# Third layer of a four-layer pair network: powers of the unscaled matrix, later lay-out copies, and a convolution border applied on VectorE

## What is computed

```
# layer 1 (the convolution and the output map; all of it linear after the windows are chosen)
g = conv3x3_same_depthwise(v, dw_w) + dw_b
out = einsum(attention_out + g, wo_w) + wo_b
# layer 2 for each image row: P = 128 positions, D = 64 channels
corr = xhat @ xhat.T / (D - 1 + 1e-6)
A = corr * (mask of the 9 largest of each row)
A = 0.5 * (A + A.T) + eye
deg = clip(A.sum(-1), 1e-6); dinv = deg ** -0.5
A = dinv[:, None] * A * dinv[None, :]
f(y) = alpha * (I - A) @ y + (A @ y) @ theta.T
y = 8 steps of a fourth-order Runge-Kutta on f;  return relu(y)
```

## Time and profile before

| | us |
|---|---|
| median of 3 runs | 1153.05 |
| lowest and highest of them | 1147.65 and 1153.18 |
| the profiled execution | 1148.3 |
| its span, first to last instruction | 1146.5 |
| layer 1, from its first product to the end of its statistics | 380.0 to 474.7 |
| layer 2, from its first product to its last lay-out sum | 478.5 to 1088.0 |

### The profile page before, as it was taken

How to read it: one execution, slowest core, us unless ns; L and a number is a source line. 1 busy time by engine, 2 the same in 40 slices (tenths; PEclk the granted TensorE clock), 3 DMA queues, 4 the chain that set the end, 5 groups by cost and what they waited for, 6 DMA issues and landing times. The chain is left out here.

```text
span 1146.5 us, 25390 instructions
## 1 busy us (share of the span) xinstructions
PE 1064.3 (93%) x9446; PEld 761.2 (66%) x9446; DVE 756.4 (66%) x3598; ACT 525.2 (46%) x1115; POOL 348.0 (30%) x481
## 2 busy tenths in 40 slices
PE   5888999999997899769999999999999999999788
PEld 3436888888886344447677776777767677776576
DVE  3685888888886322356766767667676766766268
ACT  2485777777775100125344444444445444453200
POOL 0154666666664100001212212122221212212231
PEclk9998999999999799779999999999999999999879
DMA  8000000000000000000000000000000000000012
GB/s 170 1 0 2 3 3 2 3 3 3 3 3 2 1 1 1 10 1 1 1 2 1 1 1 2 1 1 2 1 1 1 2 2 1 2 1 1 0 41 110
DMA packets 10317, 11.04 MB, mean 10 GB/s; under 512 B 3668, under 2 KB 8020, under 8 KB 10196
## 3 DMA queue, kind: packets, MB, share of 16 engines
q1 hardware_dynamic: 8820, 8.84, 3.0%
q10 hardware_dynamic: 1376, 0.59, 0.3%
HBM read 5.14 MB, written 4.19 MB: 8 GB/s over the span
## 5 line engine op out<-in xcount | busy, mean ns | idle before, releaser
L1557 PE MATMUL quad<-theta,nat 128*128 128x512 f32 x512 | 240.7, 593 | 0.0
L1356 POOL TENSOR_TENSOR nat<-nat,const 128x512 f32<-128x512 f32 x32 | 40.7, 1271 | 437.8 <-DVE nat L1495 437.8
L737 POOL TENSOR_TENSOR nat<-nat,arena 128x512 f32<-128x512 f32 x128 | 131.5, 1049 | 40.9 <-DVE arena L795 37.1
L1565 PEld LDWEIGHTS quad<-flat 128*128 128x128 f32 x768 | 104.9, 191 | 46.4 <-ACT flat L1387 25.1
L1557 PEld LDWEIGHTS quad<-theta,nat 128*128 128x128 f32 x512 | 87.5, 191 | 61.7 <-issue 61.7
L1565 PE MATMUL quad<-flat 128*128 128x128 f32 x768 | 124.2, 284 | 2.8 <-ACT flat L1387 1.7
L795 DVE CUSTOM_DVE_ANT_0 nat<-quad,arena 128x128 f32<-128x128 f32 x512 | 111.3, 283 | 1.5 <-PE quad L881 1.4
L1387 ACT ACTIVATE flat<-quad 128x256 f32<-128x256 f32 x192 | 73.6, 384 | 70.2 <-PE quad L1565 56.6
L754 ACT ACTIVATE nat<-bank 128x512 f32<-128x512 f32 x128 | 73.2, 599 | 65.1 <-PE bank L889 65.1
L1464 DVE SCALAR_TENSOR_TENSOR flat<-nat,c,duo 128x128 f32<-128x128 f32 x64 | 22.1, 345 | 102.7 <-PE duo L1574 102.7
L889 PE MATMUL bank<-const,nat 128*128 128x128 f32 x512 | 73.3, 276 | 8.1 <-ACT nat L754 8.1
(11 more groups left out here) (393 smaller groups left out, 2279.6 us busy)
## 6 DMA issues: line engine op xcount, KB each, us to landing
out<-nat SPq DMA_DIRECT2D x16, 256.0 KB, 2.0
const<-in_constants ACTq DMA_DIRECT2D x1, 400.5 KB, 3.3
arena<-in_L_conv_Ws SPq DMA_DIRECT2D x1, 240.0 KB
flat<-arena SPq DMA_DIRECT2D x3, 32.0 KB, 4.1
nat<-in_x SPq DMA_DIRECT2D x4, 0.2 KB, 12.1
arena<-in_L_conv_Wq ACTq DMA_DIRECT2D x1, 32.0 KB, 6.4
arena<-in_L_conv_Wk ACTq DMA_DIRECT2D x1, 32.0 KB, 6.1
arena<-in_L_conv_Wv ACTq DMA_DIRECT2D x1, 32.0 KB, 5.8
```

Source lines behind the costliest of these rows:

```text
L737: pool.tensor_tensor(scored, scored, of_head(least[b], h).broadcast_to([128, ROWS, L]), ALU.subtract).then_inc(lowered, 1)
L1356: pool.tensor_tensor(quarters(rem), quarters(rem), ident.unsqueeze(1).broadcast_to([128, ROWS, 128]), ALU.add).then_inc(diag_added, 1)
L1557: return pe.matmul(m.quad[:, n, :], vT[:, col(n)], m.theta[:, part, :], start=(part == 0), stop=False, skip_group_check=True)
L1565: last = pe.matmul(m.quad[:, row, place * C:(place + 2) * C], a8[g % 2][:, col(row)], zs[half][k % 2][:, n, :], start=False, stop=(k == 2) ...
```

## The change

Layer 1: the small products leave `close`. Instead, TensorE turns the eight border vectors into columns of bank 6 once, together with the bias (eight products more, ahead of `sides(2)`), VectorE copies them out, and for every bank, ahead of its statistics, VectorE subtracts the side columns in SBUF (128 x 8 elements), with two operations more for the first and the last bank.

Layer 2: write M for the unscaled matrix and D for the degrees. The kernel works with M and D^-1 in place of D^-1/2 M D^-1/2. `a1` is M with each row divided by the degree, `h2` = M D^-1 M and `h4` are the plain powers that ScalarE copies, and `a2`, `a4`, `a8` are the same divided by the degree, made on VectorE (from `h2` in SBUF), GpSimd (from `h4` in SBUF) and VectorE (from PSUM, in ScalarE's place). The turn of the scaled matrix (L1687) and the second scaling (L1541) go. GpSimd multiplies y by D^1/2 ahead (a `yn` of 128x256), and `weigh` on VectorE multiplies the result by D^-1/2. `final` is replaced by `sum_up`, two products of 64 columns for each half that accumulate onto `m.quad`, and one pair of transposes for both halves late in the step; `finish` is then two operations of 128x256. On TensorE `cor` goes ahead of `v12`, and the last `theta` goes between the first two `horner` rounds. GpSimd's `lay` comes a step later, behind the ready `a2`.

```diff
+            step(dve.tensor_copy(border, B[6][:, NWIN:NWIN + 8]))
+            step(dve.tensor_reduce(border_row, border[:, 2:8].rearrange("p (t x) -> p t x", t=2), AX.X, ALU.add))
+            sides_out = border[:, 0:2].unsqueeze(1).broadcast_to([128, 4, 2])
...
+                of_columns = out_rows(g).rearrange("p (r c) -> p r c", c=L)
+                step(dve.tensor_tensor(of_columns[:, :, 0:L:L - 1], of_columns[:, :, 0:L:L - 1], sides_out, ALU.subtract))
+                if g in (0, BANKS - 1):
+                    e = g // (BANKS - 1)
+                    outermost = of_columns[:, 3 * e, :]
+                    step(dve.tensor_scalar(outermost, outermost, border_row[:, e:e + 1], None, ALU.subtract))
+                    corners = border[:, 2 + 3 * e:5 + 3 * e:2]
+                    step(dve.tensor_tensor(outermost[:, 0:L:L - 1], outermost[:, 0:L:L - 1], corners, ALU.add))
                 dve.bn_stats(m.stats[:, 6 * g:6 * g + 6], out_rows(g))
...
                     pe.matmul(bank_of(g)[:, :], middle[:, i, :, :], m.x1[:, 4 * g:4 * g + 4, 1:1 + L],
-                              start=False, stop=False, skip_group_check=True)
-                    for dx, column in ((0, 0), (2, L - 1)):
-                        last = pe.matmul(bank_of(g)[:, column:column + 3 * L + 1:L], col_rows[:, dx, :, :], minus[:, 1:5],
-                                         start=False, stop=True, skip_group_check=True)
-
-                    if g in (0, BANKS - 1):
-                        e = g // (BANKS - 1)
-                        for dx in range(3):
-                            last = pe.matmul(bank_of(g)[:, e * 3 * L:(e * 3 + 1) * L], edge_rows[:, e, dx, :, :],
-                                             minus[:, dx:dx + L], start=False, stop=True, skip_group_check=True)
-                    last.then_inc(S("conv_made"), 1)
+                              start=False, stop=True, skip_group_check=True).then_inc(S("conv_made"), 1)
 
...
+            pe.wait_ge(S("edges_ready"), 1)
+            for n, rows in enumerate([col_rows[:, dx, :, :] for dx in (0, 2)] + [edge_rows[:, e, dx, :, :] for e in range(2) for dx in range(3)]):
+                last = pe.matmul(B[6][:, NWIN + n:NWIN + n + 1], rows, ident[C:C + 1, C:C + 1], start=True, stop=True)
             last.then_inc(S("bias_turned"), 1)
             for dx in range(3):
                 sides(2, dx)
...
+            for s in range(-1, GROUPS + 3):
                 p, c, r, a = stage(s)
+                if 0 <= s - 3 < GROUPS:
+                    pool.wait_ge(yn_weighed, min(s, GROUPS))
+                    if c is not None:
+                        pool.wait_ge(a2_ready, c + 1)
+                    lay(s - 3)
+                    pool.wait_ge(laid, s - 2)
+                if c is not None:
...
+                    pool.tensor_tensor(quarters(a4[c % 2]), quarters(h4), square_inv.unsqueeze(2).broadcast_to([128, ROWS, L]),
+                                       ALU.mult).then_inc(a4_ready, 1)
...
                     pool.wait_ge(rem_ready, p + 1)
                     pool.tensor_tensor(quarters(rem), quarters(rem), ident.unsqueeze(1).broadcast_to([128, ROWS, 128]),
                                        ALU.add).then_inc(diag_added, 1)
-                if r is not None:
...
+                    pool.wait_ge(dsq_ready, p + 1)
+                    fresh = quarters(yn[p % 2])
+                    pool.tensor_tensor(fresh, fresh, dsq.unsqueeze(2).broadcast_to([128, ROWS, C]), ALU.mult).then_inc(yn_weighed, 1)
...
-                    act.activation(a2, B[0][:, :], ACT.Copy).then_inc(a2_ready, 1)
+                    if c > 0:
+                        act.wait_ge(a4_made, c)
+                    act.activation(h2, B[0][:, :], ACT.Copy, scale=0.5).then_inc(h2_ready, 1)
...
-                    if c >= 2:
-                        act.wait_ge(final_made[1], c - 1)
-                    act.activation(a4[c % 2], B[0][:, :], ACT.Copy).then_inc(a4_ready, 1)
+                    if c > 0:
+                        act.wait_ge(a8_made, c)
+                        act.wait_ge(a4_ready, c)
+                    act.activation(h4, B[0][:, :], ACT.Copy).then_inc(h4_ready, 1)
...
-                    act.wait_ge(a8_made, c + 1)
-                    act.activation(a8[c % 2], B[0][:, :], ACT.Copy).then_inc(a8_ready, 1)
...
-            def finish(g, half):
-
-                dve.wait_ge(final_made[half], g + 1)
-                dve.scalar_tensor_tensor(out=held[half], in0=yT[g % 4][:, col(half)], scalar=m.c0[:, :], in1=B[3][:, 0:L],
-                                         op0=ALU.mult, op1=ALU.add).then_inc(held_ready[half], 1)
-                dve.wait_ge(held_ready[half], 2 * g + 1)
-                dve.tensor_tensor(held[half], held[half], B[3][:, L:2 * L], ALU.add).then_inc(held_ready[half], 1)
-                dve.wait_ge(held_ready[half], 2 * g + 2)
-                dve.scalar_tensor_tensor(out=x_of(g, half), in0=held[half], scalar=0.0, in1=x_of(g, half),
-                                         op0=ALU.max, op1=ALU.add).then_inc(x3_ready[half], 1)
+            def weigh(g, half):
+
+                dve.wait_ge(summed, 2 * g + half + 1)
+                if g > 0:
+                    dve.wait_ge(final_made, g)
+                dve.tensor_tensor(weighed[half].rearrange("p (n x) -> p n x", n=HALF), m.quad[:, HALF * half:HALF * (half + 1), 0:C],
+                                  dinv[g % 4][:, HALF * half:HALF * (half + 1)].unsqueeze(2).broadcast_to([128, HALF, C]),
+                                  ALU.mult).then_inc(weighed_ready, 1)
+
+            def finish(g):
+
+                dve.wait_ge(final_made, g + 1)
+                dve.scalar_tensor_tensor(out=held, in0=yT[g % 4], scalar=m.c0[:, :], in1=B[3][:, 0:PAIR],
+                                         op0=ALU.mult, op1=ALU.add).then_inc(held_ready, 1)
+                dve.wait_ge(held_ready, g + 1)
+                dve.scalar_tensor_tensor(out=x_of(g), in0=held, scalar=0.0, in1=x_of(g),
+                                         op0=ALU.max, op1=ALU.add).then_inc(x3_ready, 1)
+
+            def by_degree(t):
+                return t.unsqueeze(2).broadcast_to([128, ROWS, L])
 
             for s in range(-1, GROUPS + 2):
                 p, c, r, a = stage(s)
+                if c is not None:
+                    dve.wait_ge(h2_ready, c + 1)
+                    if c > 0:
+                        dve.wait_ge(v34_made, c)
+                    dve.tensor_tensor(quarters(a2), quarters(h2), by_degree(square_inv), ALU.mult).then_inc(a2_ready, 1)
...
-                    finish(r, 0)
+                    weigh(r, 0)
...
-                    finish(r, 1)
+                    weigh(r, 1)
...
+                if c is not None:
+                    dve.wait_ge(a8_made, c + 1)
+                    if c >= 2:
+                        dve.wait_ge(horner_made[1], 3 * (c - 1))
+                    dve.tensor_tensor(quarters(a8[c % 2]), quarters(B[0][:, :]), by_degree(square_inv), ALU.mult).then_inc(a8_ready, 1)
...
+                        dve.wait_ge(a4_ready, p)
+                    dve.reciprocal(square_inv, deg).then_inc(square_inv_ready, 1)
+                    dve.wait_ge(square_inv_ready, 2 * p + 1)
+                    if p > 0:
+                        dve.wait_ge(a2_made, p)
+                    for n in range(ROWS):
+                        last = dve.tensor_scalar(a1[:, col(n)], cor[:, col(n)], square_inv[:, n:n + 1], 0.5, ALU.mult, ALU.mult)
+                    last.then_inc(a1_ready, 1)
...
-                if p is not None:
-                    dve.wait_ge(b_turned, p + 1)
-                    dve.tensor_tensor(quarters(a1), quarters(B[3][:, :]), dinv.unsqueeze(2).broadcast_to([128, ROWS, L]),
-                                      ALU.mult).then_inc(a1_ready, 1)
...
+            def square(scaled, plain):
                 for n in range(ROWS):
-                    last = pe.matmul(B[0][:, col(n)], source[:, col(n)], source[:, col(n)], start=True, stop=True)
+                    last = pe.matmul(B[0][:, col(n)], scaled[:, col(n)], plain[:, col(n)], start=True, stop=True)
...
-            def final(g, half):
+            def sum_up(g, half):
 
                 pe.wait_ge(z_ready[half], 4 * g + 4)
-                pe.transpose(B[3][:, L:2 * L], zs[half][1][:, 0, :], ident)
-                for e in range(HALF):
-                    last = pe.matmul(B[3][e * C:(e + 1) * C, 0:L], zs[half][1][:, 1, e * C:(e + 1) * C], a4[g % 2][:, col(HALF * half + e)],
-                                     start=True, stop=True, skip_group_check=True)
-                last.then_inc(final_made[half], 1)
+                for n in range(HALF):
+                    row = HALF * half + n
+                    last = pe.matmul(m.quad[:, row, 0:C], a4[g % 2][:, col(row)], zs[half][1][:, n, 0:C],
+                                     start=False, stop=True, skip_group_check=True)
+                last.then_inc(summed, 1)
...
```

(41 more changed lines are left out.)

104 lines of the change are left out of this document (41 added, 63 removed).

## The result

The changed kernel takes 1143.17 us at the median of 7 runs (1137.9 to 1145.06), the kernel before, on the same chip, 1148.79 us (7 runs, 1146.61 to 1153.35). The ratio is 0.9926, with a 95% interval of 0.9907 to 0.9946: 8.5 us faster (6.2 to 10.7), where the sum of the prediction had 15.3. (The means of the two sets of runs are 8.4 us apart, the medians 5.6.) A second measurement further down, with 6 and 11 runs, gives 0.9931.

What follows compares the result with a forecast made beforehand. TensorE's own work was taken to bound layer 1 and each step of layer 2, if no other engine is late. Layer 1's -8.3 and layer 2's -7.0 gave -15.3 us; forecast 1135 us, range 1125 to 1151.

Steps and rivals of the forecast that it cites:

- third rival: Only layer 1's border change counts, hand-overs eat all of layer 2's gain: 1141 to 1146 us, chance 0.15.
- close: Layer 1: without the small products a pair of banks takes 1.72 us instead of 3.17, -11.7 us in all.
- the stall: Layer 1: TensorE waits once for bank 0, delayed by VectorE's new operations, +1.0 us (0 to 1.5).
- The three small operations of VectorE: Layer 1, bank 0: ahead of its statistics, each waited for, at some 0.25 us, 0.75 together.
- The added one-column products: Layer 1: eight more products on TensorE with nothing to hide them, +1.9 us.
- The first part of a step: Layer 2: `v12` at 2.71, second `horner` at 3.70, late `theta` pair at 10.24 us; -0.15 us a step.
- The second part of a step: Layer 2: reordered `horner`, `theta` and transposes take 2.82 us instead of 2.93, -0.11 us a step.
- The ends of layer 2: The layer's end gets longer by a chain of sum, multiply, turn and two operations: +0.8 us.
- the first and the second rival: Layer 2: scan stretched or `a2` late, 1145 to 1151 us, chance 0.13; scan stopped for GpSimd's multiply, 1170 us, chance 0.08.

Runs made afterwards that it cites:

- matrix_only: The kernel before with the new layer 2 alone, layer 1 as before: 1145.8 us, 0.9956 of the kernel before.
- best: Changed kernel with border and bias vectors turned by one product, next xs turn before the last horner, bank 1 evacuated before bank 0's border: 1128.88 us, 0.9829.
- cor_behind: The changed kernel with the products of `cor` moved back behind `v12`: 1161.74 us, 1.0111 of the kernel before.
- thin_twice: The kernel before with its eight one-column bias products issued twice in a row, nothing else: 1153.03 us, 1.0033 of the kernel before.
- border_only: The kernel before with the new layer 1 alone, layer 2 as before: 1145.12 us, 0.9951 of the kernel before.
- xs_in_gap: The changed kernel with the next group's turn of xs moved ahead of a step's last `horner`: 1136.74 us, 0.9891 of the kernel before.
- lay_free: The changed kernel without GpSimd's wait for `a2` ahead of the copies of `lay`: 1148.3 us, 0.9991 of the kernel before.

## Why the prediction was right, and where it was not

The time, 1143.2 us, lies in the range and, by under a microsecond, in the forecast's own one (1125 to 1144), and the sign and the places of the gain were right. It lies in that of the third rival as well (1141 to 1146); only `matrix_only` decides between them. The sum was too large by some 7 us: layer 1 gave 5.7, just outside its bounds of 6 to 10, and layer 2 gave 3.3, just inside its own of 3 to 11, so that the width of the range, and not the sum, kept the time inside it. By its own steps:

- **`close`** was to give 11.7 us with 1.0 and 0.5 given back on VectorE. From the first `close` to the end of the statistics the trace has 50.5 us instead of 60.7: 10.2 less, as forecast, though with errors that cancel: a pair takes 1.82 us and not 1.72 wherever it stands behind `sides`, six times of eight (1.72 holds where it follows another pair, as in the rows of `best`), and the stall costs 0.7 and not 1.0; the rest must lie in the tail, which I have not taken apart. The three small operations of VectorE took 0.17, 0.29 and 0.17 us and 0.73 from the first one's start to the statistics (423.58 to 424.31), close to the 0.75 that I had put.
- **The added one-column products** cost 1.8 us on TensorE (forecast 1.9) and, behind them, 1.7 us of the clock, which the sum did not have. This is the missing term of layer 1. The rows that I priced them by the earlier trace rows show the pace of 16 records, and I took it that twice as many cost twice as much.
- **The front of layer 1** took 1.0 us more up to the one-column products (30.7 against 29.7). That isn't the change: `matrix_only`, which has the old layer 1, took 30.4, and so did the second profile of the changed kernel.
- **The first part of a step** came out to within 0.02 us at `v12` and at the late `theta` pair (0.06 late at the second `horner`), and `cor_behind` shows that the chain to `a2` was the right reason for `v12`.
- **The second part of a step** is the step that failed in layer 2: 2.94 us instead of 2.82. The wait of 1.08 between the last two rounds was right. But the last `horner` behind a wait takes 0.55 us to the next start, and not 0.44. The earlier trace rows had shown it: the round that follows the short wait at 788.65 is listed with 0.71 us and not 0.61, and I had myself put it at 0.55 for the kernel before. By 30 steps this is 3.3 us, nearly all of the 3.7 that layer 2 gave less than forecast, and half of what the whole sum was too large by. A step gives 0.13 us, not 0.26.
- **The ends of layer 2.** Together they cost about 0.7 us where 0.8 were forecast, but by errors that cancel. The last group's tail was to cost 0.8 and gave 0.45 (from the last `v12` to the aggregation 24.88 us, not 25.33), and the step ahead of it gave 0.2; its chain of small operations was priced too high. The start, which I had not priced, cost 1.3. The first `v12` starts 30.9 us behind the aggregation and not 30.1: the first square stands 0.14 later, with VectorE's scaling of the first `a1` slowed from 0.87 to 1.23 us beside GpSimd's multiply of y, and from the square to `v12`, which there waits for VectorE's `a2`, it takes 0.66 more. The second `v12` follows after 17.13 us and not 16.59; in that step TensorE waits 0.33 us for GpSimd's diagonal and 0.47 for ScalarE ahead of the last `horner`, and did not wait before. In a full step the longer scaling is hidden.
- **The rivals.** The searches take 279 to 286 ns on average by line where they took 277 to 284, and the longest of all 298 where it was 297, so that the first and the second rival fall at their mechanism. GpSimd's own multiply took 1.04 us, not 1.27.

## What to carry to other kernels

Price a wait together with what follows it: on TensorE the group behind a wait took 0.1 us longer as well (its weight loads began with its products and not ahead of them, as the rows of the step show; no run changed this alone), and a dependent round leaves a gap that independent short work can fill (0.22 us a step here). When an operation moves onto the path between two products, move something independent between them as well, and look at what other engines do beside it. Turn row vectors together, by one transfer and one product, rather than one column at a time.

## What the runs showed of the hardware

- Products of one column brought TensorE's clock from 2.4 to 1.2 GHz although the engine was listed as busy the whole time: in none of the two kernels with 16 such records (`matrix_only` and the one before), in all seven profiles with 32 of them (the changed kernel twice, `thin_twice`, `border_only`, `xs_in_gap`, `cor_behind`, `lay_free`), and for 10 us when the later ones stood between dense products. The busy share of TensorE says nothing about this; only the clock's column shows it.
- A VectorE operation with a single tensor in SBUF was slowed by GpSimd. The scaling of `cor` by four instructions of 128x128 took 0.87 us in the kernel before, with GpSimd idle, and 1.23 us beside the multiply of y. The mean of 368 ns instead of 283 hides how: in a step three of the four take 0.27 to 0.29 us, and the second takes 0.64, from 800.32 until just behind the end of GpSimd's multiply (800.88). By the Trainium skill (SBUF — State Buffer, Who interferes with whom) `tensor_scalar` can enter a mode that uses the ports that are shared with GpSimd; the slowed scaling agrees. The same section says that an instruction with at most one input in SBUF, outside such modes, does not contend. It does not name the searches; here they have one input each, and GpSimd's multiply left them as they were.
- In the kernel before, two operations of `finish` show the difference beside GpSimd's diagonal multiply (799.78 to 801.05). The first has one input in SBUF and one in PSUM, the second has both in SBUF, and alone each takes 0.29 us:

```profile
799.93 0.29 DVE L1467 TENSOR_TENSOR flat<-flat,duo 128x128 f32<-128x128 f32 x1
800.26 0.94 DVE L1469 SCALAR_TENSOR_TENSOR flat<-flat 128x128 f32<-128x128 f32 x1
```

- A multiply of 128x512 with both inputs in SBUF took 0.99 us beside GpSimd's copies and 0.69 without them.
- A gap that an engine spends on a wait for another can be listed as "issue": the 0.28 and 0.62 us ahead of `v12` in `lay_free` and `cor_behind` end with VectorE's multiply.
